# A language-model tower on one core: the expert stage in 20 tiles of four 32-token blocks in place of 24 tiles of two 64-token blocks, with a shorter plan and a refilled opening

## The reference

```
emb = word[x] + npi[..] + posi[..] + seg[..] + modal[..] + time2vec(age) + time2vec(delays)
x   = layer_norm(emb)
q, k, v = split(x @ qkv_w.T + qkv_b); q, k = rms_norm(q), rms_norm(k)      # 12 heads of 16
x   = softmax(q @ k.T / 4) @ v @ proj_w.T + proj_b                         # with residual and norm around
logits = normed @ w_router; probs = softmax(logits); e = argmax(probs)
priority = cumsum(onehot(e), axis=tokens); keep = priority <= 64           # capacity per sequence and expert
y   = relu(normed @ wi[e]) @ wo[e]          # wi 192x768, wo 768x192, float32
out = x + max(probs) * (y where kept, normed elsewhere)
```

## Time and profile before

| what | before |
| --- | --- |
| median of 3 runs | 388.18 us (387.72 to 389.49) |
| profiled execution | 388.62 us |
| its span, first to last instruction | 386.9 us |
| PE busy | 337.5 us (87%) |
| DVE busy | 258.0 us (67%) |
| POOL busy | 198.4 us (51%) |
| ACT busy | 160.9 us (42%) |
| mean granted TensorE clock | 0.901 of full speed |
| weight copies L1185 on DVE | 96, 69.7 us |

### The profile page before, as it was taken

How to read it: one execution, slowest core, us unless ns; L and a number is a source line. 1 busy time by engine, 2 the same in 40 slices (tenths; PEclk the granted TensorE clock), 3 DMA queues, 4 the chain that set the end, 5 groups by cost and what they waited for, 6 DMA issues and landing times.

```text
span 386.9 us, 8606 instructions
## 1 busy us (share of the span) xinstructions
PE 337.5 (87%) x3170; PEld 217.8 (56%) x3170; DVE 258.0 (67%) x742; ACT 160.9 (42%) x299; POOL 198.4 (51%) x191
## 2 busy tenths in 40 slices
PE   8989679689899999989999724799999999999980
PEld 3435446556677776667777412265556655566550
DVE  7774937864779799996767677745666556655520
ACT  3634334514366665647556320233433334333320
POOL 5776374585268661037101255645765676666421
PEclk9566968955999999999999986899999999999995
DMA  4438921113627873371424390494222211122100
GB/s 91 108 86 224 238 66 44 45 34 50 189 32 160 229 146 90 113 195 55 135 65 122 114 255 0 112 278 129 54 57 54 61 57 35 58 55 60 30 2 0
DMA packets 35066, 37.96 MB, mean 98 GB/s; under 512 B 6214, under 2 KB 32531, under 8 KB 35022
## 3 DMA queue, kind: packets, MB, share of 16 engines
q1 hardware_dynamic: 25680, 24.20, 21.7%
q0 software_dynamic: 8768, 12.63, 15.0%
q10 hardware_dynamic: 576, 0.59, 0.5%
HBM read 30.97 MB, written 7.21 MB: 99 GB/s over the span
## 4 chain that ended last, share of the span: by engine, by line
PE 60%; DVE 20%; issue 7%; POOL 4%; ACT 3%; DMA 2%; POOLq 0%; DVEq 0%; ACTq 0%
PE psum L1488 13%; PE psum L1467 9%; PE psum L1238 6%; PE psum L1239 5%; PE psum L1472 5%; PE psum L1479 4%; PE psum L1294 4%; PE psum L1308 4%; POOL weights L392 2%; DVE small L835 2%; PE psum L1459 2%; PE psum L1374 2%; PE psum L1232 1%; DMA weights<-pair_rows,ids 1%; DVE weights L794 1%
## 5 line engine op out<-in xcount | busy, mean ns | idle before, releaser
L1185 DVE COPY shared<-weights 128x1152 f32 x96 | 69.7, 769 | 10.9 <-issue 10.2
L522 POOL DMA_INDIRECT tower_out<-shared,oidx x24 | 36.2, 1507 | 37.3 <-DVE shared L1199 34.7
L1488 PE MATMUL psum<-shared 128*64 128x192 f32 x576 | 52.1, 330 | 0.9 <-ACT shared L716 0.9
L1488 PEld LDWEIGHTS psum<-shared 128*64 128x64 f32 x576 | 39.2, 137 | 19.4 <-issue 13.8
L1199 DVE SCALAR_TENSOR_TENSOR shared<-psum,shared 128x192 f32<-128x192 f32 x24 | 10.0, 418 | 47.1 <-PE psum L1488 47.1
L1467 PE MATMUL psum<-shared 128*64 128x384 f32 x192 | 36.8, 505 | 0.5 <-ACT shared L708 0.5
L1238 PE MATMUL psum<-shared,weights 96*128 96x192 f32 (+1 forms) x96 | 36.0, 460 | 0.7 <-ACT weights L574 0.7
L916 DVE TENSOR_REDUCE guard<-psum 128x12 bf16<-128x1536 f32 x16 | 28.1, 1754 | 10.9 <-PE psum L1294 10.9
L712 ACT ACTIVATE shared<-psum 128x768 f32<-128x768 f32 x24 | 19.5, 812 | 37.6 <-PE psum L1472 37.6
L431 POOL TENSOR_TENSOR small<-small,mhalf 128x2 f32<-128x2 f32 x16 | 12.3, 771 | 44.1 <-DVE small L843 44.0
L1239 PE MATMUL psum<-shared,weights 97*128 97x192 f32 (+1 forms) x96 | 33.0, 428 | 0.0
(11 more groups left out here) (196 smaller groups left out, 714.8 us busy)
## 6 DMA issues: line engine op xcount, KB each, us to landing
weights<-in_wo SPq DMA_DIRECT2D x16, 576.0 KB, 6.9
weights<-in_wi SPq DMA_DIRECT2D x32, 192.0 KB, 4.8
weights<-in_wi SPq DMA_DIRECT2D x32, 96.0 KB, 5.2
token_rows<-shared SPq DMA_DIRECT2D x14, 192.5 KB
tower_out<-shared SPq DMA_DIRECT2D x14, 96.0 KB
token_rows<-shared ACTq DMA_DIRECT2D x2, 192.5 KB, 3.0
blk_token<-expert_lists,blk_entry POOLq DMA_INDIRECT x24, 2.5
shared<-token_rows,blk_token POOLq DMA_INDIRECT x24, 3.3
```

The source lines that it names most:

```text
L522: G.indirect_dma_start(out=out, out_offset=bass.IndirectOffsetOnAxis(ap=oidx[q % 2][:, :], axis=0), in_=res[q % 2], in_offset=None, bounds ...
L1185: V.tensor_copy(w_now[q % 2][k][:, lo:hi], weights[:, bass.ds(at[k] + lo, hi - lo)]).then_inc(sem(("wi_now", "wo_now")[part]), 1)
L1488: last = T.matmul(psum[q % 2][k * BT:(k + 1) * BT, 3, 0:D], hidT[:, c * P + k * BT:c * P + (k + 1) * BT], w_now[q % 2][k][:, WI_COLS + c * ...
```

## The change

The expert stage gets 80 blocks of 32 tokens, four to a tile, 20 tiles. `w_now` has four buffers, one set. DVE copies the weights of blocks 0 to 2, with three column loads, ACT those of block 3 (`take_last`, `last_column`) after all 19 plan steps. On DVE wo copies of tile q now stand behind the wi copies of q+1 and ahead of result(q-1). The plan has nine steps up to `blk_entry`, on arrays of 320 elements; `blk_col` comes after it with a semaphore of its own. One rank step per batch goes, one moves forward, and `place` uses another bank from the second batch on. SP loads 12 with 10 and 11, and 14 and 15 without the wait on `rows2`. In the opening, `keep` has more matmuls at the start and in turns 2, 3, 4 and 10; ACT does `xn_in(1)` ahead of `exp_scores(0, 0)`, and its table of exponentials is loaded in turn 1; DVE's list of turn 2 is reordered; POOL's gathers and powers interleave in another order.

```
-BT = P // 2
+NB = 4
+BT = P // NB
-        w_now = [[share_b(WCOL) for _ in range(2)] for _ in range(2)]
+        w_now = [share_b(WCOL) for _ in range(NB)]
...
# SP
-            for e in (10, 11):
+            for e in (10, 11, 12):
                 load_expert(e)
             sp.wait_ge(sem("p_logit0"), NPAIR)
             sp.wait_ge(sem("p_logit1"), NPAIR)
-            sp.wait_ge(sem("rows2"), 16)
-            for e in (12, NE - 2, NE - 1):
-                load_expert(e)
+            load_expert(NE - 2)
+            load_expert(NE - 1)
...
# POOL
-            gather_terms(2, (0, 1, 2, 3))
+            gather_terms(2, (0, 1, 2))
             p1(1)
+            gather_terms(2, (3,))
             gather_terms(3, (0,))
             p2(1)
-            gather_terms(3, (1, 2, 3))
+            gather_terms(3, (1, 2))
             p1(2)
-            gather_terms(4, (0, 1))
+            gather_terms(3, (3,))
             p2(2)
-            gather_terms(4, (2, 3))
+            gather_terms(4, (0, 1, 2, 3))
...
# ACT
+                if t in (2, 3):
+                    xn_in(t - 1)
                 if live(t - 2):
                     exp_scores(t - 2, 0)
-                if t == 2:
-                    xn_in(1)
...
+            def take_last(q, part):
+                lo, hi = ((0, WI_COLS), (WI_COLS, WCOL))[part]
+                freed(act, sem(("b_hid", "b_y")[part]), q)
...
+                S.copy(w_now[NB - 1][:, lo:hi], weights[:, bass.ds(last_at[q % 2] + lo, hi - lo)]).then_inc(
+                    sem(("wi_last", "wo_last")[part]), 1)
...
+            act.wait_ge(sem("plan"), N_PLAN)
+            last_at = [last_column(0), None]
+            take_last(0, 0)
+            take_last(0, 1)
             turn_rows(0)
             relu(0)
             for q in range(NTILE):
                 if q + 1 < NTILE:
+                    last_at[(q + 1) % 2] = last_column(q + 1)
+                    take_last(q + 1, 0)
                     turn_rows(q + 1)
                 turn_hid(q)
+                if q >= 1:
+                    take_last(q, 1)
                 if q + 1 < NTILE:
                     relu(q + 1)
...
# DVE, turn 2
+                if t == 2:
+                    es(1)
...
                     add_times(5)
-                    plain_rows(1)
-                    es(1)
-                    gd(0, 0)
                     ed(1)
                     st2(1)
+                    gd(0, 0)
+                    sh2(1)
                     add_times(6)
-                    sh2(1)
                     add_times(7)
-                    gd(0, 1)
                     plain_rows(2)
                     es(2)
+                    gd(0, 1)
...
# DVE, expert stage
             def columns(q):
-                return [dve.value_load(blk_col[k * BT:k * BT + 1, q:q + 1], ...) for k in range(2)]
+                return [dve.value_load(blk_col[k * BT:k * BT + 1, q:q + 1], ...) for k in range(NB - 1)]
...
             for q in range(NTILE):
                 if q + 1 < NTILE:
-                    at = columns(q + 1)
-                    take_weights(q + 1, 0)
+                    at[(q + 1) % 2] = columns(q + 1)
+                    take_weights(q + 1, 0, (0, 1, 2))
                 if q >= 1:
+                    take_weights(q, 1, (0, 1, 2))
                     result(q - 1)
-                if q + 1 < NTILE:
-                    take_weights(q + 1, 1)
...
# PE
             def pe_turn(t):
+                if t in (3, 4):
+                    keep(psum_q[0], 3)
...
+                if t in (2, 3):
+                    keep(psum_q[0], 4)
                 if live(t - 1):
                     tx(t - 1)
...
-                    keep(psum_q[0], 2)
+                    keep(psum_q[0], 5 if t == 2 else 2)
                     gs(t - 2, 1)
...
             def hidden(q):
...
                 for b in range(2):
-                    for k in range(2):
+                    for k in range(NB):
                         T.matmul(hid_ps[k * BT:(k + 1) * BT, b, :], gT[:, b * P + k * BT:b * P + (k + 1) * BT],
-                                 w_now[q % 2][k][:, b * WI2:(b + 1) * WI2], start=True, stop=False)
+                                 w_now[k][:, b * WI2:(b + 1) * WI2], start=True, stop=False)
```

More of the change, by code:

```diff
@@ L67, in tower_kernel @@
 def tower_kernel(nc, t, out):
-    assert NBLK == 48 and NTILE == 24
+    assert NBLK == 80 and NTILE == 20
     ctx = ExitStack()
@@ L132, in tower_kernel @@
         bases = share_a(NSEQ * NE).rearrange("p (n e) -> p n e", e=NE)
[L133 removed]
+        rank_a = share_a(8 * NE).rearrange("p (n e) -> p n e", e=NE)
+        rank_b = share_a(8 * SPLIT).rearrange("p (n k) -> p n k", k=SPLIT)
         chosen = share_a(2 * P)[:, 0:8 * NE // 2].bitcast(BF16).rearrange("p (n e) -> p n e", e=NE)
@@ L675, in act_turn @@
                     sines(7)
+                    S.activation(cols(small[1], ZSUM + 1, 1), round_up[:, 0:1], ACT.Exp, scale=0.0)
                 if live(t - 2):
@@ L1167, in _ @@
+            planned(V.tensor_reduce(length, big2, AX, ALU.add))
+            V.scalar_tensor_tensor(blk_entry[:, :], length, list_step[:, 0:1], nth, ALU.add, ALU.add).then_inc(sem("blk_entry"), 1)
             planned(V.tensor_reduce(ej, big, AX, ALU.add))
[L1168 to L1172, removed]
@@ L1173, in _, with take_weights @@
-            planned(V.scalar_tensor_tensor(length, ej, float(SPLIT), within, ALU.mult, ALU.add))
-            planned(V.tensor_scalar(late, half_pos[:, 0:1].broadcast_to([P, NTILE]), float(NLISTS), None, ALU.mult))
-            V.tensor_tensor(blk_entry[:, :], length, late, ALU.add).then_inc(sem("blk_entry"), 1)
-            def take_weights(q, part):
+            V.tensor_scalar(blk_col[:, :], ej, float(WCOL), None, ALU.mult).then_inc(sem("blk_col"), 1)
+            def take_weights(q, part, blocks):
@@ L1186, in take_weights @@
                         sem(("wi_now", "wo_now")[part]), 1)
             def columns(q):
-                return [dve.value_load(blk_col[k * BT:k * BT + 1, q:q + 1], min_val=0, max_val=(NE - 1) * WCOL) for k in range(2)]
+                return [dve.value_load(blk_col[k * BT:k * BT + 1, q:q + 1], min_val=0, max_val=(NE - 1) * WCOL) for k in range(NB - 1)]
             def result(q):
@@ L1200, in result @@
                                        ALU.mult, ALU.add).then_inc(sem("res"), 1)
-            dve.wait_ge(sem("blk_entry"), 1)
+            dve.wait_ge(sem("blk_col"), 1)
             dve.wait_ge(sem("weights"), 80 * ARENA_FIRST)
-            at = columns(0)
-            take_weights(0, 0)
+            at = [columns(0), None]
+            take_weights(0, 0, (0, 1))
+            planned(V.scalar_tensor_tensor(within, ej, -float(SPLIT), length, ALU.mult, ALU.add))
+            planned(V.scalar_tensor_tensor(within, within, 1.0, nth, ALU.subtract, ALU.add))
             planned(V.tensor_tensor(big, over(expert_iota[:, :]), ej.unsqueeze(2).broadcast_to([P, NTILE, NE]), ALU.is_equal))
@@ L1327, in at @@
                     for b, (first, count) in enumerate(BATCHES):
-                        if first + count == 2 * i:
+                        if b == 0 and first + count == 2 * i:
                             pe.wait_ge(sem("bases"), first + count + 1)
-                            pe.wait_ge(sem("rank"), RANK_STEPS * b + 4)
+                            pe.wait_ge(sem("rank"), RANK_STEPS * b + 5)
                 for h in range(HEADS):
```

92 lines of the change are left out of this document (57 added, 35 removed).

## The result

The changed kernel takes 393.35 us (median of 4 runs, 392.43 to 394.04), the kernel before 387.95 beside it (386.11 to 389.49): the ratio is 1.014, with a 95% interval of 1.009 to 1.019. It is slower, by more than the 0.5% that can be told from no change. Forecast were 391 us and slower; the range was 382 to 399. The profiled execution took 393.65 us, 5.0 more than the one before, and its span is 391.9.

What follows compares the result with a forecast made beforehand. PE was taken to set the expert stage before, DVE after, at 6.95 us a tile. 388.62 + 10.0 (expert stage) + 1.5 (last experts' loads) - 9.0 (opening) = 391.1, called 391 us; range 382 to 399.

Steps and rivals of the forecast that it cites:

- rival B: Expert tile: column loads cost their records' 0.71 us, periods shorter by 0.4 to 0.5; total 383 us; chance 0.12.
- Rival C: Expert tile: loads overlap the copies after all and PE sets a 5.45 us period; total 363 us; chance 0.04.
- rival D: Expert stage: PE's 1.5 us idle in every tile brings the clock down; +17, total 408 us; chance 0.08.
- period of 7.05: Expert tile: if DVE copies fully locked out GpSimd, POOL's tile would be 7.05 us and the sum 2 us higher.
- most of the load is over when the gathers come: Stage start: early loads of the last three experts delay the first gathers only a little; +1.5 us taken.
- hidden(0) held by ACT's copies: Stage start, a sign of being right: ACT's last-block copies, after 19 plan steps, put hidden(0) at 247.2, before 244.51.
- Rival E: Start caught by the transfers (+5 in place of +1.5) and opening gives 7; total 396.5 us; chance 0.12.
- The plan's -1.2: Start of the expert stage: fewer plan steps up to blk_entry, on smaller arrays, save 1.2 us.
- tx(1) 51.20 to 47.6, -3.6: Opening, turn 2: xn_in(1) goes ahead of table load and exponentials, DVE reaches its first guard sooner; tx(1) 3.6 us earlier.
- stays at 2.4: Opening, turn 2: fillers keep the clock at 2.4 GHz until tg(0,1), another 3.4 us, 59.51 to 52.5.
- Turn 3: Opening: POOL's eight gathers cause a 3.4 us PE idle, the clock falls to 0.50; tg(1,1) 87.57 to 79.5, -8.1.
- rival A: Opening: the clock holds through turn 3, 5.2 us less; total 386 us; chance 0.17.

Runs made afterwards that it cites:

- loads ahead: Changed kernel with VectorE's three column loads moved ahead of the previous tile's result, behind the six weight copies: 367.60 us, ratio 0.943.
- old wait: Changed kernel with experts 12, 14 and 15 again loaded only after the third row gather: 392.08 us, ratio 1.006.
- ten fillers: Changed kernel with 10 instead of 14 filler matmuls (`keep`) at the start, as before the change: 392.56 us, ratio 1.013.
- combination: Changed kernel with loads ahead of the result, ACT not waiting for the whole plan, ten fillers, only experts 14 and 15 after the first row gather: 359.14 us.
- no wait for the plan: Changed kernel, loads ahead of the result, experts 12, 14, 15 after the first row gather, ACT starting once blk_col is written: 364.22 us, ratio 0.940.
- opening alone: Kernel before the change with only the new opening, expert stage still in 24 tiles: 382.63 us, ratio 0.984.
- late experts after the first row gather: Changed kernel with loads ahead of the result and experts 12, 14 and 15 loaded after the first row gather: 365.06 us, ratio 0.941.

## Why the prediction was right

**The expert tile.** The step that decides held: the order puts three loads where nothing covers them, DVE sets the tile, PE idles at a clock of 1.00. Forecast were 6.95 us, measured 6.83 (6.89 as the mean). The copies took the forecast 4.15 from their start to oidx, which with its semaphore took 0.25 for 0.15 to 0.2; from there to the next copies are 2.43 us for 2.65 (306.04 to 308.47). That is 0.81 a load for 0.88, and as a load added costs 0.76, some 0.15 of it is not the loads': the price by their records, rival B's 0.71, was the nearer one. Run of six to run of six is what the loads' move cut to 5.35 on average, PE's period, and what doubling them raised to 9.06 on average. Rival C is what the kernel would have been with the loads ahead: 363 was its price, 367.60 the run.

**The clock in the expert stage (rival D).** It stayed at 1.00 with idles of 1.43 us in each tile, and D did not come. With the loads doubled, and idles of 3.56 to 3.93 us, it did swing. The swing between the two levels that the Trainium skill describes (TensorE: Matmul & The Clock Gate, A second HAM failure mode: psum-queue depth-cycling) did not show in the changed kernel; the swing in that run stands behind idles more than twice as long.

**POOL.** The scatter fell into DVE's idle and took 1.00 us in place of 1.72. The period of 7.05 that the prediction worked out from the rule of the Trainium skill (SBUF — State Buffer, SBUF: two separate sides) did not come: a row gather beside the six copies took 1.47 us at the median, where it had taken 1.08, and with the loads ahead POOL ran beside copies in tiles of 5.35.

**The start.** Here two terms were mis-sized and one step was wrong in its order. ACT's copies of the last block were to hold hidden(0), with transfers mostly hidden behind them, "most of the load is over when the gathers come", +1.5. In fact the scatters and two gathers were slow enough to end after ACT: rows at 242.90, ACT at 240.12. So the sign "hidden(0) held by ACT's copies" failed. The run with the old wait parts the two: there ACT does hold hidden(0), 11.06 us behind blk_entry, 3.0 more than before for a forecast of 3.9, and the transfers add 3.65 for 1.5. Together +6.67 for +5.4: an error in each direction. Rival E had the mechanism right, a start caught by the transfers and an opening that gives less, at a smaller size than its 396.5. The plan's -1.2 came at -1.17, partly by luck: its first two steps grew from 0.42 to 0.69 us each, which was not in the sum, and one of the steps that went had 0.55 and not 0.18.

**The opening.** -9 was forecast, -5.96 measured in the profiled execution. The step that failed is the first, "tx(1) 51.20 to 47.6, -3.6": it came at 50.38, -0.8. Those behind it held. The turn "stays at 2.4": from tx(1) to tg(0,1) are 4.96 us, for 4.9 forecast and 8.31 before. Turn 3 gave 1.6 for 1.1, and the turns after it 0.2 for 0.9. What the prediction left out is the work ahead of turn 2. The projections now ran at the higher clock, so PE came sooner to a norm of DVE that it has to wait for, 2.11 us where it had waited 0.56, and behind this wait the clock was 0.50 for 6.5 us. In the changed kernel's trace the slower time matmuls come on top. In the four traces without them tx(0) is at 29.1 to 29.3 as before, the wait 2.8 to 3.3 us, and tx(1) at 48.9 to 49.1. The run with ten fillers shows the forecast opening nearly to the tenth (tx(1) 47.61, tg(0,1) 52.58, last slot 9.0 sooner). But the combination, with ten fillers too, waited 2.99 us at that norm and had tx(1) at 50.38, so that the four fillers are the cause is not shown.

Turn 3 went as said: a fall near 75 to 80 and 0.50 for 20 us, so rival A is out. The idle ahead of it was 1.84 us and not 3.4, and it was a wait for DVE: POOL's eight gathers took their 10 us (65.12 to 75.13), but no PE idle stands behind them in this trace. But the size of this term isn't sharp. With the same opening the last slot was done at 225.4 to 225.6 in three traces (changed kernel, old wait, doubled loads), at 224.1 to 224.5 in three (loads ahead, no wait for the plan, and opening alone, which has the old rank steps) and at 222.7 in one (late experts after the first row gather): gains of 6 to 9 us.

**The end.** The stage took 138.18 for 139.1: hidden(0) to hidden(3) 0.5 less than worked out, the sixteen periods behind it 1.0 less (110.21 for 111.2), and the rest, where output(19) waits for wo copies that wait for output(18), 0.55 more. The last 0.97 lies behind the issue of the last scatter, from whose end to the end of the span are 7.43 us for 8.40 before; its cause stays open.

**The sum.** The opening gave 3.0 us less than forecast and the start took 1.3 more; the stage and the end gave 0.9 and 1.0 back. So the total came 2.4 us off where the terms were up to 3 off, and that it came this near is in part luck. "Slower" had a chance of 0.50, and what made it so is the expert tile, which was read rightly: with its loads moved the kernel is faster than before.

## What to carry to other kernels

A register load on a compute engine's queue is cheap only where its engine still has work in flight; behind an instruction that waits for its own engine, three of them cost 2.4 us in every tile. So when a tile is cut into more blocks, count the sequencer's work for each block, and look which instruction stands ahead of it. And a transfer that no longer waits for its turn is not free: find what shares its queues, then look who needs its data, since what is taken from the one may come back at the other.

## What the runs showed that was not expected

In the changed kernel's trace the granted clock says nothing before its first change. It reads 1.00 for the first 40 us, but ACT's sine steps, which follow the time matmuls, come every 2.57 us there, as they do in the trace before where the clock reads 0.50:

```profile
11.16 0.90 ACT L566 ACTIVATE shared<-psum,round_up 128x768 f32<-128x768 f32 x1 [1.60 <-PE psum L1484]
...
13.73 0.90 ACT L566 ACTIVATE shared<-psum,round_up 128x768 f32<-128x768 f32 x1 [0.94 <-PE psum L1484]
```

```profile
9.80:19.60 9.80, 9.80 (x17) 5.14 (x16) 5.64 (x11) 5.63 (x7) 7.67 (x8) 1.00 0.40 105
```

So this trace's mean of 0.927 is too high. In the trace before, the first two such steps were 1.23 us apart (7.65 and 8.88), at the higher clock, and then the clock fell. In three of the seven traces with the new opening as it is in the change that short fast piece is missing, and they are the three with the latest last slot. The combination's trace, with ten fillers, lacks it too and has its last slot at 225.54. One profiled execution therefore shows the opening to about 3 us only; a change of that size there needs several.
